# Maxima of the second attention carried into a spare row of the turned queries; maxima of the first written in one step

## The reference

```python
# layer 0: attention without weights, q = norm(x), k = v = ctx, 16 heads of 16 features
# layer 0: feed-forward with ternary weights, a 3-tap convolution, silu, integer activations
# layer 1: attention with weights
qp, kp, vp = relu(q @ Wq.T), relu(k @ Wk.T), relu(v @ Wv.T)
E = 0.25 * einsum('bqhd,bkhd->bhqk', qh, kh)      # 16 heads, 128 x 128 scores for each sequence
out = einsum('bhqk,bkhd->bqhd', softmax(E, axis=-1), vh)
# layer 1: feed-forward with 8 experts, of which each token uses 2
```

## Time and profile before

| | us |
|---|---|
| median of 3 runs | 1877.53 (1872.9 to 1878.95) |
| the profiled execution, its own time | 1878.45 |
| its span, first to last instruction | 1876.7 |

### The profile page before, as it was taken

One profiled execution on the slowest core, in us unless ns is written; L12 is line 12 of the kernel. 1 busy time (PEld: TensorE's weight loads), 2 busy tenths in 40 slices (PEclk: granted clock), 3 DMA queues, 4 the chain that ended last, 5 costly groups with the idle time before them and its releaser, 6 DMA issues. The chain is left out here.

```text
span 1876.7 us, 49808 instructions
## 1 busy us (share of the span) xinstructions
PE 1596.0 (85%) x20058; PEld 1094.2 (58%) x20058; DVE 1554.4 (83%) x2977; ACT 1184.8 (63%) x1916; POOL 865.1 (46%) x932
## 2 busy tenths in 40 slices
PE   0799999856766766748999999996899999999998
PEld 0577777624444444435777777775466666665665
DVE  7799999857888888876888888886888888888885
ACT  1789889778777787716888888886233333333332
POOL 1455555427777777753333333332233333333332
PEclk9999999979999999969999999998899999999999
DMA  9200000000000000000002000000121211212211
GB/s 313 92 3 3 3 3 3 3 0 1 1 1 1 1 1 1 1 17 2 3 2 70 3 2 3 3 3 1 59 100 58 102 69 57 103 68 71 100 57 68
DMA packets 45526, 68.11 MB, mean 36 GB/s; under 512 B 6273, under 2 KB 36737, under 8 KB 45313
## 3 DMA queue, kind: packets, MB, share of 16 engines
q1 hardware_dynamic: 42944, 65.03, 10.3%
q10 hardware_dynamic: 2368, 0.02, 0.1%
HBM read 56.39 MB, written 8.65 MB: 35 GB/s over the span
## 5 line engine op out<-in xcount | busy, mean ns | idle before, releaser
L719 ACT ACTIVATE a_exp<-a_score_t 128x1024 f32<-128x1024 f32 x256 | 262.1, 1024 | 81.8 <-PE a_score_t L526 81.7
L641 DVE TENSOR_REDUCE a_maxes<-a_score 128x8 f32<-128x1024 f32 x256 | 311.2, 1216 | 0.6 <-PE a_score L509 0.6
L1547 POOL TENSOR_TENSOR e_a_parts<-e_act,e_a_parts 128x512 f16<-128x512 f32 x128 | 153.3, 1198 | 329.1 <-ACT e_a_parts L1518 329.1
L1518 ACT ACTIVATE e_a_parts<-e_act 128x512 f16<-128x512 f32 x128 | 80.6, 630 | 303.0 <-DVE e_act L1350 269.0
L1095 POOL TENSOR_TENSOR b_hidden<-b_hidden,b_shifted 128x508 f32<-128x508 f32 x128 | 161.6, 1262 | 119.3 <-DVE b_hidden L945 119.3
L1232 PE MATMUL e_up_ps<-e_n_turned,e_up_t 128*128 128x512 f16 x768 | 187.9, 381 | 8.5 <-DVE e_act L1346 8.5
L1246 PE MATMUL e_out<-e_down_t,e_a_parts 128*128 128x256 f16 x1536 | 188.4, 273 | 0.8 <-POOL e_a_parts L1547 0.8
L1232 PE MATMUL e_gate<-e_n_turned,e_gate_t 128*128 128x512 f16 x768 | 187.9, 381 | 0.2 <-issue 0.2
L1246 PEld LDWEIGHTS e_out<-e_down_t,e_a_parts 128*128 128x128 f16 x1536 | 149.6, 98 | 39.0 <-POOL e_a_parts L1547 1.1
L1102 POOL TENSOR_TENSOR b_hidden<-b_hidden,b_scales 128x512 f32<-128x512 f32 x128 | 168.2, 1318 | 3.0 <-ACT b_scales L1077 3.0
L780 POOL TENSOR_TENSOR a_split<-ctx,a_split 128x256 f16<-128x256 f32 x64 | 43.0, 672 | 268.6 <-ACT a_split L736 268.6
(11 more groups left out here) (206 smaller groups left out, 4027.5 us busy)
## 6 DMA issues: line engine op xcount, KB each, us to landing
ctx<-e_weights SPq DMA_DIRECT2D x64, 512.0 KB, 5.4
out<-x SPq DMA_DIRECT2D x16, 512.0 KB, 2.9
x<-in_x SPq DMA_DIRECT2D x3, 2048.0 KB, 19.0
ctx<-in_ctx SPq DMA_DIRECT2D x1, 4096.0 KB, 27.0
ctx<-in_ctx SPq DMA_DIRECT2D x1, 3072.0 KB, 16.5
a_exp<-in_L_ffn_w SPq DMA_DIRECT2D x2, 1024.0 KB, 9.6
x<-in_x SPq DMA_DIRECT2D x1, 1536.0 KB, 16.4
ctx<-in_ctx SPq DMA_DIRECT2D x1, 1024.0 KB, 13.5
```

What stands on the lines that cost most here:

```text
L641: nc.vector.tensor_reduce(maxes[:, p * PAIRS:(p + 1) * PAIRS], score[:, :].rearrange("p (h k) -> p h k", k=P), AX.X, ALU.max).then_inc(max ...
L719: nc.scalar.activation(exp32[:, u % 2, 2 * p:2 * p + 2, :], score_t[:, :].rearrange("p (g n) -> p g n", g=2), ACT.Exp, scale=DH ** -0.5 / ...
L1547: nc.gpsimd.tensor_tensor(a_parts[:, e % 4, 1, :], act3[:, e % 2, :], a_parts[:, e % 4, 0, :], ALU.subtract).then_inc(alo_ok, 1)
```

## The change

Second attention: the maxima no longer go through 16 extra matmuls per tile. The constant column in `k_stack`'s fourth slot becomes `scale * scale`; after the maxima are turned and copied (now 16 partitions), SP issues two DMAs per tile that write the 16 rows of negative maxima into `q_turned`, row 48 of each head's 64 rows. `do_scores_t` is then 8 matmuls a pass and waits, for pass 0, for these two DMAs. The two passes change places: the first slot of step i now holds pass 1 of tile i - EL - 1, the second slot pass 0 of tile i - EL, on PE and ACT alike. `spread` is not built. The experts' weights are loaded in 27 pieces, one for each step from step 32 on, behind that step's two DMAs in SP's list.

First attention: the maxima are written by the reduction itself into `neg_max`, in float16, and the sign moves into `spread` (fill -1); the scaling instruction (L693) and its signal go, and PE waits for the second reduction instead.

```diff
+FIRST_PIECE = 32
+
+MOVED = (False, True)
...
+    moved = MOVED[layer]
+    unit = scale * scale if layer else -1.0
+
+    passes = ((EL + 1, 1), (EL, 0)) if moved else ((EL, 0), (EL, 1))
...
-        spread = sb("spread", [P, PAIRS, P], F16)
+        if not moved:
+            spread = sb("spread", [P, PAIRS, P], F16)
         spread_made = sem("spread_made")
 
         def make_spread(pool):
-
-            nc.gpsimd.memset(spread[:], scale * scale).then_inc(spread_made, 1)
+            if moved:
+                return
+            nc.gpsimd.memset(spread[:], unit).then_inc(spread_made, 1)
...
-        maxes = sb("maxes", [P, HEADS], F32)
-        neg_max = sb("neg_max", [P, 2, 2, SLOT], F16)
-        neg_max_t = sb("neg_max_t", [P, 2, P], F16)
+        if layer:
+            maxes = sb("maxes", [P, HEADS], F32)
+
+        neg_max = sb("neg_max", [P, 2, 2, PAIRS if moved else SLOT], F16)
+        neg_max_t = sb("neg_max_t", [HEADS if moved else P, 2, P], F16)
+        largest = lambda u: neg_max[:, u % 2, :, 0:PAIRS].rearrange("p r (a k) -> p a r k", k=HG)
...
-            nc.vector.memset(k_stack[:, :, :, 3, 0:1], 1.0).then_inc(made, 1)
+            nc.vector.memset(k_stack[:, :, :, 3, 0:1], unit if moved else 1.0).then_inc(made, 1)
...
-            if layer:
-
-                @block.sync
-                def _(sp):
-                    sp.wait_ge(cl_ok, 3 * EXPERTS)
-                    load_experts(nc, sp, io, m)
+            @block.sync
+            def _(sp):
+                def step(t, u):
+                    if moved:
+                        sp.wait_ge(m_copied, t + 1)
+                        for half in range(2):
+                            row = half * SLOT + 3 * DH
+                            sp.dma_start(q_turned[row:row + 1, u % 4, :, :],
+                                         neg_max_t[half * PAIRS:(half + 1) * PAIRS, u % 2, :]).then_inc(max_in[half][u % 2], 16)
+                    if layer and t >= FIRST_PIECE:
+                        if t == FIRST_PIECE:
+                            sp.wait_ge(cl_ok, 3 * EXPERTS)
+                        load_experts(nc, sp, io, m, t - FIRST_PIECE)
+
+                write_steps(step, UNROLL, TILES, 0)
+                if layer:
+                    for loaded in m.expert_loaded[0:3]:
+                        sp.wait_ge(loaded, 16 * EXPERTS)
+                    sp.wait_ge(m.expert_loaded[3], 48)
...
-                    reach(pe, neg_ok, t + 1)
-                    nc.tensor.transpose(neg_turned, neg_max[:, u % 2, :, :].rearrange("p r n -> p (r n)"),
-                                        m.ident16[:, :]).then_inc(m_turn, 1)
...
+                    if p == 0 and moved:
+                        for half in range(2):
+                            reach(pe, max_in[half][u % 2], 16 * (t // 2 + 1))
+                    elif p == 0:
                         reach(pe, m_copied, t + 1)
                     reach(pe, exp_ok, t * 2 + p)
                     for k in range(HG):
                         for half in range(2):
                             h, _ = head_of(2 * p + half, k)
                             r = SLOT * half
-                            nc.tensor.matmul(score_t[:, column(half, k)], k_turned[r:r + SLOT, u % 4, h // 2, :],
-                                             q_turned[r:r + SLOT, u % 4, h // 2, :], start=True, stop=False)
-                        for half in range(2):
+                            last = nc.tensor.matmul(score_t[:, column(half, k)], k_turned[r:r + SLOT, u % 4, h // 2, :],
+                                                    q_turned[r:r + SLOT, u % 4, h // 2, :], start=True, stop=moved)
+                        for half in range(0 if moved else 2):
                             h, _ = head_of(2 * p + half, k)
                             r = SLOT * half
                             last = nc.tensor.matmul(score_t[:, column(half, k)], spread[r:r + SLOT, h // 2, :],
...
+                    def scores_t_pass(n):
+                        lag, p = passes[n]
+                        if inside(i - lag, TILES):
+                            do_scores_t(i - lag, (u - lag) % UNROLL, p)
...
-                    if run_exps:
-                        do_scores_t(i - EL, uE, 0)
+                    scores_t_pass(0)
                     if layer and run_out:
                         turn_out(i - FL)
...
-                    if run_exps:
-                        do_scores_t(i - EL, uE, 1)
+                    scores_t_pass(1)
...
-                def take_max(t, p):
+                def take_max(t, u, p):
                     reach(dve, scores_ok, t * 2 + (p + 1))
-                    nc.vector.tensor_reduce(maxes[:, p * PAIRS:(p + 1) * PAIRS], score[:, :].rearrange("p (h k) -> p h k", k=P),
-                                            AX.X, ALU.max).then_inc(max_ok, 1)
+                    if layer:
+                        nc.vector.tensor_reduce(maxes[:, p * PAIRS:(p + 1) * PAIRS], score[:, :].rearrange("p (h k) -> p h k", k=P),
+                                                AX.X, ALU.max).then_inc(max_ok, 1)
+                    else:
+                        nc.vector.tensor_reduce(largest(u)[:, p, :, :], score[:, :].rearrange("p (r k n) -> p r k n", r=2, n=P),
+                                                AX.X, ALU.max).then_inc(max_ok, 1)
 

...
-                        take_max(i - SL, 1)
+                        take_max(i - SL, uS, 1)
+                    if layer and run_scores:
                         reach(dve, max_ok, (i - SL) * 2 + 2)
-                        nc.vector.tensor_scalar(neg_max[:, uS % 2, :, 0:PAIRS].rearrange("p r (a k) -> p r a k", k=HG),
-                                                maxes[:, :].rearrange("p (a r k) -> p r a k", r=2, k=HG), -1.0 / (scale * scale), None,
+                        nc.vector.tensor_scalar(largest(uS), maxes[:, :].rearrange("p (a r k) -> p a r k", r=2, k=HG), -1.0 / (scale * scale), None,
                                                 ALU.mult).then_inc(neg_ok, 1)
...
+                    def exp_pass(n):
+                        lag, p = passes[n]
+                        if inside(i - lag, TILES):
+                            do_exp(i - lag, (u - lag) % UNROLL, p)
...
+def load_experts(nc, sp, io, m, n):
+
+    if n < 2 * EXPERTS:
+        name = ("L1_ffn_gate_proj", "L1_ffn_up_proj")[n // EXPERTS]
+        sp.dma_start(m.expert_raw[n // EXPERTS][:, n % EXPERTS, :], io[name][n % EXPERTS]).then_inc(m.expert_loaded[n // EXPERTS], 16)
+    elif n < 3 * EXPERTS:
+        sp.dma_start(m.expert_raw[2][:, n % EXPERTS, :].rearrange("p (c i) -> p c i", c=DC),
+                     io["L1_ffn_down_proj"][n % EXPERTS].rearrange("(c p) i -> p c i", p=P)).then_inc(m.expert_loaded[2], 16)
```

More of the change, by code:

```diff
@@ L372, in make_spread @@
             nc.gpsimd.affine_select(out=spread[:], in_=spread[:], pattern=[[-1, PAIRS], [0, P]],
-                                    compare_op=ALU.not_equal, fill=scale * scale, base=-SLOT, channel_multiplier=1).then_inc(spread_made, 1)
+                                    compare_op=ALU.not_equal, fill=unit, base=-SLOT, channel_multiplier=1).then_inc(spread_made, 1)
             pool.wait_ge(spread_made, 3)
@@ L408, in attention_stage @@
         q_copied, k_copied, m_copied = sem("q_copied"), sem("k_copied"), sem("m_copied")
+        max_in = [[sem(f"max_in{half}_{n}") for n in range(2)] for half in range(2)]
         scores_ok, max_ok, neg_ok = sem("scores_ok"), sem("max_ok"), sem("neg_ok")
@@ L494, in turn_maxima @@
                 def turn_maxima(t, u):
-                    reach(pe, neg_ok, t + 1)
-                    nc.tensor.transpose(neg_turned, neg_max[:, u % 2, :, :].rearrange("p r n -> p (r n)"),
-                                        m.ident16[:, :]).then_inc(m_turn, 1)
+                    if layer:
+                        reach(pe, neg_ok, t + 1)
+                    else:
+                        reach(pe, max_ok, (t + 1) * 2)
+                    nc.tensor.transpose(neg_turned, neg_max[:, u % 2, :, :].rearrange("p r n -> p (r n)"), m.ident16[:, :]).then_inc(m_turn, 1)
                 def do_scores(t, u, p):
@@ L671, in step @@
                     if run_scores:
-                        reach(dve, neg_ok, i - SL)
-                        take_max(i - SL, 0)
+                        if layer:
+                            reach(dve, neg_ok, i - SL)
+                        take_max(i - SL, uS, 0)
                     if not layer and inside(i - STATS, TILES):
@@ L722, in step @@
                 def step(i, u):
-                    run_exps = inside(i - EL, TILES)
-                    uE = (u - EL) % UNROLL
+                    def exp_pass(n):
+                        lag, p = passes[n]
+                        if inside(i - lag, TILES):
+                            do_exp(i - lag, (u - lag) % UNROLL, p)
                     if not layer and isinstance(i, int) and i in (0, head - 1):
@@ L743, in step @@
```

(28 more changed lines are left out.)

8 lines of the change are left out of this document (4 added, 4 removed).

## The result

The changed kernel takes 1882.54 us, the median of 13 runs (1880.82 to 1885.13), beside 1878.6 us for the kernel before in its 13 runs: a ratio of 1.0027, 95% interval 1.0018 to 1.0035. It is slower, though by little; the forecast was 1869.7. The profiled execution's span is 1879.1 us where it was 1876.7.

The account below looks back on a forecast made before the run. It took PE to bound the second attention, busy 50.00 of 50 us, with DVE's chain next. Terms of 6.5 + 1.0 + 1.2 - 0.5 = 8.2 us less gave 1869.7 us, with 8 in 10 from 1853 to 1879.

Parts of the forecast that it names:

- Matmuls removed: 0.22 us a pass.: Second attention, transposed scores: dropping 8 of 16 matmuls saves PE 0.22 us a pass, 0.44 a step.
- What is late next: the keys' low part.: Second attention: DVE's chain ending in the keys' low part holds the key turn, so PE can use 0.11 of 0.44 us.
- The query turn's wait for the splits' copy: Second attention: with PE sooner, the query turn waits for DVE's copy of the splits, making it 0.12 us later.
- From the key turn to the next split turn PE has nothing removed.: Second attention: this stretch of PE's step keeps its length, so a step goes from 6.81 to 6.70 us.
- The term of 6.5 us: Second attention's loop: 59 steps, each 0.11 us shorter, give 6.5 us; ends 0 and 26 us.
- The rival "no gain in the loop": Second attention: the 0.11 us a step is lost in PE's stops; 1.7 us less remain, 1876 us; chance 0.18.
- The two DMAs: 1.85 us, cost nothing.: Second attention: both transfers of maxima land in 1.85 us, 0.64 before the second slot, hidden at no cost.
- The sentence on the Trainium skill: Second attention's two DMAs: the skill's fixed part of about 2.0 us gives 2.4 us, still inside by 0.1.
- The rival of late DMAs: Second attention: the DMAs come late and set the step from 2.81 us on; 1880 or 1898 us; chance 0.13.
- The end of the pipeline: +0.5.: Second attention's end: the last tile's DMAs lie open and one pass follows later; 0.5 us lost, between 0 and 1.85.
- Preparation: -1.0.: Preparation: without POOL building `spread` beside it, a DVE instruction gains 0.9 us, a smaller memset 0.1; ends 0 and 1.1.
- First attention: -1.2.: First attention: dropping the scaling gains 1.2 us at 6 turns of DVE's hardware loop, nothing in plain steps; ends 0 and 3.

Follow-up runs that it names:

- this part alone: Only the first attention's part of the change, the second attention's extra matmuls put back, against the kernel before: 1877.96 us, ratio 1.0004.
- the early low part: Changed kernel with the maxima turned in full width and the keys' low part moved to the front of DVE's step: 1866.39 us, ratio 0.9941 to before.
- the pieces last: Changed kernel with all 27 pieces of experts' weights issued behind the last tile's two DMAs, none inside the loop: 1886.86 us, ratio 1.0061 to before.
- the old order: Changed kernel with pass 0 of a tile left in the first slot and pass 1 in the second: 2101.91 us, ratio 1.1199 to before.
- the second attention's part alone: Only the second attention's part of the change, the first attention's scaling instruction and waits kept, against the kernel before: 1880.11 us, ratio 1.0015.

## Why the prediction was wrong, step by step

- *Matmuls removed: 0.22 us a pass.* Right. The passes start 0.33 us ahead of what follows in the changed kernel (1101.22 to the output turn at 1101.55) and in the later ones.
- *What is late next: the keys' low part.* Right, and shown by taking the link away: 6.71 to 6.49 us. The query turn's wait for the splits' copy, put at 0.12, is 0.12.
- *"From the key turn to the next split turn PE has nothing removed."* True, but something was added, and this is the first of two steps that failed. The turn of the maxima became a narrow one, which costs 0.10 us more, on the very chain on which I counted a gain of 0.11: key turn to splits' copy is 4.00 us (1097.33 to 1101.33), where it was 3.90 (1002.20 to 1006.10). I had read the copy's shape with its 16 partitions and not asked what it makes of the matmul. The term of 6.5 us is 0.3. The full-width turn gives the forecast's step back, so the cause of the longer step is shown. The rival "no gain in the loop" was this case, with a loss that I laid at the wait instead of at a matmul.
- *The two DMAs: 1.85 us, cost nothing.* The second step that failed, and by what its repair gives back the larger one. The landing is mis-sized: 2.48 to 2.50 us. Issuing takes 0.65 us each (1.31 for two), not 0.28 + 0.05, and the landing behind it about 1.8, not 1.47: the row of the experts' weights was the nearest, but that transfer goes to DRAM and its issue is one of another shape. The sentence on the Trainium skill ("DMA: Bandwidth & Descriptors", "Anatomy of one DMA — SWDGE (gpsimd) path") came out at 2.4; for the sum of these two the runs agree with it, not with my rows. That is luck of the sum: an estimate by the same page for one DMA alone is 0.05 + 2.0 = 2.05, and it takes 1.66. With 2.49 the slot at 1103.59 - 1100.98 = 2.61 us leaves 0.12 to spare in place of 0.64, and any slower landing shows. Five of 59 did: +3.8 us. The rival of late DMAs had them late in all steps from 2.81 on; in fact the ordinary one is in time and single ones are not. I had priced the typical landing, not the slowest.
- *The end of the pipeline: +0.5.* It was +1.0, three landings open at 0.90, 0.92 and 1.43 us.
- *Preparation: -1.0.* Right, -1.03. The rows of the kernel after:

```profile
829.13 0.27 DVE L219 TENSOR_TENSOR mean<-stats 128x64 f32<-128x64 f32 x1 [0.30 <-PEq L906]
...
830.15 0.23 DVE L228 TENSOR_TENSOR rstd<-rstd,root 128x64 f32<-128x64 f32 x1
```

The 0.23 us stand where 1.12 stood, with POOL idle beside it. The Trainium skill ("SBUF — State Buffer", "Who interferes with whom") has it that a DVE instruction with two inputs in SBUF contends with a GpSimd instruction that reads SBUF; this pair of rows agrees.

- *First attention: -1.2.* The mechanism is there, the gain isn't shown. At the turn of the hardware loop the copy now follows its matmul at once (L525 ends at 202.59, the copy starts at 202.63; 0.18 before). But the stage gains 0.3 us between these profiles, loses 0.3 in the kernel with this part alone, and differs by 1.5 between two profiles of the same code.

```profile
202.36 0.23 PE L525 MATMUL a_turn<-ident,a_neg_max 128*128 128x128 f16 x1
...
202.63 0.23 DVE L704 COPY a_neg_max_t<-a_turn 128x128 f16<-128x128 f16 x1
```

Term by term, in the profiles: the loop brings 0.3 us instead of 6.5, late landings take 3.8 instead of nothing, the end 1.0 instead of 0.5, and the first attention brings 0.3 instead of 1.2. That is 11.4 us of the distance; stages that nothing was forecast for give 1.1 back. Neither repair alone reaches the forecast of 1869.7: the full-width turn gives 1878.09 us (ratio 1.0001), one DMA 1873.21 (0.9985), where the changed kernel has 1.0027.

Open: whether the packets of instructions make the landings late or only go with them, and why the landings come later than the packets alone would have it. The changed kernel's five late steps come back at the same steps of the loop in the kernel with the full-width turn (and one more), four of them in the one with the early low part (and three others) and in the one with the pieces last, three in the one with the old order, one in the one with the second attention's part alone (and two others). One DMA, in both profiles that have it, is not late at all: its last semaphore update comes 1.61 us behind the copy, and in no step of the loop more than 0.1 us after that, so the slack of about 0.95 us (1.66 against a slot of 2.61) did not have to hide a late landing.

## What to carry to other kernels

When an edit shrinks a tile, ask what it makes of each matmul that writes it: here a narrower one between full ones cost 0.10 us more, and on a chain a tenth of a microsecond a step is the whole gain. A transfer that is hidden needs slack for its slowest landing, not for its median, and two small DMAs in one queue are one issue slower than a single one. Before removing work from the engine that is full, move the result that arrives just behind it: here the step went from 6.81 to 6.71 us by the removal, and to 6.49 by that move.

## What the runs showed of the hardware

- A turn of the form `128*16` between matmuls of `128*128` held PE for 0.16 us from start to start, the same turn as `128*128` for 0.07; the step differs by 0.10 us.
- A small DMA on SP from SBUF to SBUF takes 0.65 us to issue for one row (2 KB), 0.50 for both rows in one (4 KB), and the latter lands 1.66 us behind the end of its source's copy; two in a row land 2.49 us behind it.
- In the six kernels with two DMAs a tile, 26 of 28 late steps had a packet of the kind `instruction` (8 or 16 KB) that began 1.3 to 2.1 us behind the end of the copy, and 5 of the 326 others.
- With a wait of PE of 2.18 us in each step of 10.3 us the granted clock was 0.59 to 0.69 in the 4 us behind it; the wait and the clock cost 3.5 us a step in all.
